# A conditioned EMA block and a top-k FFN on one core: where the scores are made, warm-up matmuls, and a new order of steps

## The reference, cut to what matters

```python
ctx    = ema(x, tau_ctx)                                  # scan over the 32 tokens
wg     = sigmoid([x, ctx] @ Wg.T + bg);  gated = x * wg
mod    = 0.5 + sigmoid(gelu(x @ Wn1.T + bn1) @ Wn2.T + bn2)   # 128 modes
temporal = sum_d softmax(blend)[d] * ema(gated * mod[d], tau[d])
gate   = sigmoid(temporal @ Wtemp.T + btemp)
y      = layernorm((gelu(x @ Wsoma.T + bsoma) * gate) @ Wout.T) * gamma + beta
scores = y @ w_router
top 16 of the 32 tokens of each sequence:
    out[token] = y[token] + sigmoid(score) * (gelu(y[token] @ W1 + b1) @ W2 + b2)
result = x + out
```

## Time and profile before

| | |
|---|---|
| median of three runs | 192.11 us (189.43, 192.11, 192.43) |
| the profiled execution | 189.27 us, its span 187.5 us |
| mean granted clock of TensorE | 0.991 of full speed |
| TensorE matmuls busy | 172.6 us, 92% |
| VectorE / GpSimd / ScalarE busy | 143.6 / 134.8 / 96.5 us |

### The profile page before, as it was taken

How to read it: one execution, slowest core, us unless ns; L and a number is a source line. 1 busy time by engine, 2 the same in 40 slices (tenths; PEclk the granted TensorE clock), 3 DMA queues, 4 the chain that set the end, 5 groups by cost and what they waited for, 6 DMA issues and landing times.

```text
span 187.5 us, 3480 instructions
## 1 busy us (share of the span) xinstructions
PE 172.6 (92%) x1154; PEld 130.4 (70%) x1154; DVE 143.6 (77%) x223; ACT 96.5 (51%) x177; POOL 134.8 (72%) x158
## 2 busy tenths in 40 slices
PE   5798999999999999999999999999999983994991
PEld 4485445877669588695769687688689943983881
DVE  1628897769997988859787887798789749858822
ACT  3548697264680141772505454578487465157030
POOL 7838000788897999979686988999797599529800
PEclk9999999999999999999999999999999997899999
DMA  5687000000000000000000000000002000303032
GB/s 128 167 209 201 0 3 0 0 2 5 0 0 0 3 0 3 0 0 0 3 2 0 0 3 2 0 0 3 2 0 59 0 2 0 112 3 112 0 112 59
DMA packets 12785, 5.62 MB, mean 30 GB/s; under 512 B 2880, under 2 KB 12640, under 8 KB 12768
## 3 DMA queue, kind: packets, MB, share of 16 engines
q1 hardware_dynamic: 11904, 5.20, 10.3%
q10 hardware_dynamic: 864, 0.20, 0.5%
HBM read 3.30 MB, written 2.10 MB: 29 GB/s over the span
## 4 chain that ended last, share of the span: by engine, by line
PE 76%; DVE 11%; issue 3%; POOL 3%; ACT 2%; DMA 2%; ACTq 0%; DVEq 0%; POOLq 0%
PE ring L1042 27%; PE ring L1109 6%; PE ring L1015 5%; PE ring L1026 4%; PE ring L999 4%; PE ring L978 4%; PE ring L1000 4%; PE ring L1049 4%; DVE small L842 3%; PE ring L1057 3%; DVE spread L846 3%; PE ring L1006 2%; PE ring L1032 2%; PE ring L992 2%; PE ring L966 2%
## 5 line engine op out<-in xcount | busy, mean ns | idle before, releaser
L468 POOL TENSOR_TENSOR ctx_acc<-ctx_acc,prod 128x256 f32<-128x256 f32 (+17 forms) x75 | 81.0, 1095 | 30.9 <-DVE prod L817 26.8
L817 DVE TENSOR_TENSOR prod<-ring,gm 128x256 f32<-128x256 f32 (+17 forms) x75 | 41.3, 577 | 8.9 <-PE ring L1042 7.4
L1042 PE MATMUL ring<-mod_hi,decayed_lo 128*128 128x512 f32 (+15 forms) x104 | 35.0, 374 | 0.0
L1042 PE MATMUL ring<-mod_lo,decayed_hi 128*128 128x512 f32 (+15 forms) x104 | 30.1, 326 | 0.0
L1042 PE MATMUL ring<-mod_hi,decayed_hi 128*128 128x512 f32 (+15 forms) x104 | 30.0, 327 | 0.0
L1042 PEld LDWEIGHTS ring<-mod_hi,decayed_lo 128*128 128x128 f32 x104 | 18.4, 189 | 7.6 <-issue 6.3
L1042 PEld LDWEIGHTS ring<-mod_lo,decayed_hi 128*128 128x128 f32 x104 | 19.2, 189 | 2.0 <-issue 1.2
L1042 PEld LDWEIGHTS ring<-mod_hi,decayed_hi 128*128 128x128 f32 x104 | 19.2, 189 | 0.9
L804 DVE TENSOR_TENSOR state<-ring,blend_w 128x1024 f32<-128x1024 f32 x16 | 18.8, 1219 | 1.1 <-PE ring L1015 0.9
L1109 PE MATMUL ring<-w_sb,gm 128*128 128x128 f32 x128 | 15.8, 282 | 0.1
L1109 PEld LDWEIGHTS ring<-w_sb,gm 128*128 128x128 f32 x128 | 15.4, 199 | 0.3 <-issue 0.3
(11 more groups left out here) (168 smaller groups left out, 358.9 us busy)
## 6 DMA issues: line engine op xcount, KB each, us to landing
x_nat<-in_x_dram SPq DMA_DIRECT2D x3, 512.0 KB, 4.2
out_dram<-x_nat SPq DMA_DIRECT2D x3, 512.0 KB, 3.2
x_nat<-in_x_dram SPq DMA_DIRECT2D x2, 256.0 KB, 4.7
w_sb<-in_L_ffn_W_dram SPq DMA_DIRECT2D x2, 256.0 KB, 5.3
out_dram<-x_nat SPq DMA_DIRECT2D x2, 256.0 KB, 3.2
down<-in_cond_dram SPq DMA_DIRECT2D x2, 64.0 KB, 2.7
prod<-in_L_cond_Wg_dram ACTq DMA_DIRECT2D x1, 128.0 KB, 2.8
prod<-in_L_cond_Wsoma_dram ACTq DMA_DIRECT2D x1, 64.0 KB, 2.9
```

Source lines behind the costliest of these rows:

```text
L468: nc.gpsimd.tensor_tensor(dst, dst, packed(prod[:, n % NP, 0:width(r)], r, k), ALU.add).then_inc(acc_done, 1)
L817: nc.vector.tensor_tensor(dst, packed(slot(step), r, k), lagged(gated(r), r, k), ALU.mult).then_inc(read(step), 1)
L1042: last = nc.tensor.matmul(to[:, c], w[:, k, :], src[:, c], start=(i == 0), stop=(i == len(parts) - 1))
```

## The change

1. Scores: `var` on GpSimd no longer adds 1e-5 in an instruction of its own; `squares` has a 129th column that holds 1e-5, and the sum takes it in. GpSimd makes the score product right after the power. `score` on VectorE copies the product into PSUM and makes `spread` from there; `pick_w` likewise reads its sigmoid from a copy in PSUM. The step `score` now takes the bank, and `bc` uses the same one; the equality test overwrites the spread scores there, after the greater-than test instead of before it. The bank comes free after `pick_w` instead of after `pick`.
2. `normed` on ScalarE waits for the power, scales `o_sb` first and does the tanh last.
3. Warm-up matmuls: 5 before the steps, 1 after `turn_b`, 4 after `turn_a`.
4. The four DMAs of `bn1` are issued ahead of `bias_in` and of x of round 1. The biases are halved in step `soft`.
5. A new `ORDER`.

```diff
-WARM = 3
+WARM = (5, 1, 4)
 ORDER = """
+decay:0 powers:0 xt:0 turn_b:0 turn_a:0 h1:0 context:0 mod:0 soft:0 turn_c:0 xt:1 wg:0 xt:2 decays:0
+context:1 xt:3 context:2 split:0 h1:1 wg:1 gated:0 rw:0 context:3 turn_f:0 gated:1 table:0.0 table:0.1
...
+unit:4.2 unit:4.6 up:1.0 state:4.0 plus_beta:1 gate:3 up:1.1 score:2 normed:2 residual:1 soma_gate:3
+unit:4.4 turn_pick:1 bc:2 tie:2 pick:2 down:1 out:3.0 stats:3.0 gather:2 out:3.1 stats:3.1 var:3 unit:4.8
+unit:4.15 carry:4.0 up:2.0 back:4.0 up:2.1 sum:4 score:3 normed:3 bc:3 scatter:1 turn_pick:2 tie:3
+plus_beta:2 pick:3 gate:4 soma_gate:4 down:2 gather:3 residual:2 out:4.0 stats:4.0 scatter:2 var:4
+plus_beta:3 up:3.0 score:4 up:3.1 residual:3 normed:4 bc:4 turn_pick:3 plus_beta:4 tie:4 pick:4 down:3
+gather:4 scatter:3 up:4.0 up:4.1 turn_pick:4 down:4 residual:4 scatter:4
...
+        def scores(r, i):
+            return slot(("score", r, 0))[:, NT * T + i * NT:][:, 0:tiles(r)]
...
+            for g in range(BT):
+                sp.dma_start(bn1[g * HN:(g + 1) * HN, :], col(b_n1)).then_inc(bn1_in, 16)
             sp.dma_start(bias_in[:, 0:1], col(b_g)).then_inc(bias_inn, 16)
             sp.dma_start(bias_in[:, 1:2], col(b_n2)).then_inc(bias_inn, 16)
             sp.dma_start(tiles_of(x_nat, 1), tiles_of(x_dram, 1)).then_inc(x_in[1], 16)
-            for g in range(BT):
-                sp.dma_start(bn1[g * HN:(g + 1) * HN, :], col(b_n1)).then_inc(bn1_in, 16)
...
                 elif kind == "var":
-                    nc.gpsimd.tensor_scalar(small[..4..], small[..5..], 1e-5, None, ALU.add)
-                    nc.gpsimd.tensor_tensor(small[..7..], small[..4..], minus_half[..], ALU.pow)
+                    nc.gpsimd.tensor_tensor(small[..7..], small[..5..], minus_half[..], ALU.pow)
+                    pool.wait_ge(rstd_done, r + 1)
+                    for h in range(QUADS[r]):
+                        pool.wait_ge(read(("out", r, h)), reads_after(("out", r, h)))
+                    nc.gpsimd.tensor_tensor(small[..6..], o_sb[:, r % 2, 0:tiles(r), E], small[..7..], ALU.mult)
...
                 elif kind == "score":
-                    dve.wait_ge(rstd_done, r + 1)
-                    nc.vector.tensor_tensor(s[6], o_sb[:, r % 2, 0:tiles(r), E], s[7], ALU.mult)
+                    for former in FORMER[step]:
+                        dve.wait_ge(read(former), reads_after(former))
                     dve.wait_ge(score_done, r + 1)
+                    nc.vector.tensor_copy(scores(r, 0), small[:, r % 2, 6, 0:tiles(r)])
                     nc.vector.tensor_tensor(spread[:, 0:tiles(r), :], eye_t[..],
-                                            s[6][:, :, None].to_broadcast([P, tiles(r), T]), ALU.mult)
+                                            scores(r, 0)[:, :, None].to_broadcast([P, tiles(r), T]), ALU.mult)
...
                 elif kind == "pick":
+                    nc.vector.tensor_copy(scores(r, 1), small[:, r % 2, 9, 0:n])
                     nc.vector.scalar_tensor_tensor(out=pick_w[:, 0:n, :],
-                        in0=small[:, r % 2, 9, 0:n][..], scalar=1.0,
+                        in0=scores(r, 1)[:, :, None].to_broadcast([P, n, SEL]), scalar=1.0,
                         in1=pick[:, 0:n, 0:SEL], op0=ALU.add, op1=ALU.mult)
...
+                if kind in ("turn_b", "turn_a"):
+                    warm_up(WARM[1 if kind == "turn_b" else 2])
```

More of the change, by code:

```diff
@@ L59 @@
 ORDER = """
[L60 to L79, removed]
@@ L80 @@
-soma_gate:4 normed:3 turn_pick:2 plus_beta:2 pick:3 down:2 plus_beta:3 residual:2 out:4.0 gather:3 stats:4.0
-var:4 scatter:2 turn_pick:3 up:3.0 up:3.1 score:4 bc:4 normed:4 tie:4 pick:4 down:3 plus_beta:4 residual:3
-gather:4 scatter:3 up:4.0 residual:4 up:4.1 turn_pick:4 down:4 scatter:4
+decay:0 powers:0 xt:0 turn_b:0 turn_a:0 h1:0 context:0 mod:0 soft:0 turn_c:0 xt:1 wg:0 xt:2 decays:0
+context:1 xt:3 context:2 split:0 h1:1 wg:1 gated:0 rw:0 context:3 turn_f:0 gated:1 table:0.0 table:0.1
+table:0.2 wg:2 low:0 gated:2 table:0.3 mod:1 split:1 low:1 wg:3 gated:3 early:0 unit:0.0 h1:2 unit:0.8 h1:3
@@ new lines @@
+turn_d:0 unit:0.12 unit:0.1 unit:0.7 nat:0.0 unit:0.14 unit:1.0 unit:1.13 early:1 unit:1.14 unit:1.6 ffn_w:0
+unit:0.13 mod:2 turn_e:0 unit:1.7 plus_beta:0 unit:0.5 unit:1.15 nat:1.0 unit:0.4 state:0.0 unit:0.2 soma:0
+unit:1.1 unit:0.6 unit:0.10 state:1.0 soma:1 unit:0.9 carry:0.0 unit:0.11 unit:1.8 unit:0.15 unit:0.3
+split:2 low:2 back:0.0 sum:0 mod:3 nat:1.1 unit:1.2 unit:2.0 unit:2.13 unit:1.11 state:1.1 unit:2.9 gate:0
+soma_gate:0 unit:2.1 unit:1.5 unit:1.3 early:2 nat:2.1 out:0.0 unit:2.2 xt:4 context:4 unit:1.10 carry:1.1
@@ new lines @@
+state:2.1 unit:1.9 carry:1.0 unit:2.8 back:1.1 unit:1.12 nat:2.0 h1:4 stats:0.0 unit:2.11 early:3 unit:1.4
+state:2.0 split:3 low:3 carry:2.1 back:1.0 soma:2 unit:2.7 nat:3.0 unit:2.12 unit:3.0 unit:2.14 unit:3.5
+nat:3.1 unit:2.6 unit:3.15 sum:1 unit:3.1 state:3.1 unit:2.3 carry:2.0 unit:3.8 unit:2.4 var:0 state:3.0
+gate:1 back:2.1 carry:3.1 soma_gate:1 unit:2.15 unit:2.5 back:2.0 unit:2.10 unit:3.10 mod:4 split:4 wg:4
+low:4 score:0 out:1.0 gated:4 unit:3.13 unit:4.0 unit:4.10 unit:4.5 sum:2 stats:1.0 bc:0 back:3.1 normed:0
@@ new lines @@
+unit:3.2 tie:0 out:1.1 stats:1.1 var:1 unit:4.7 pick:0 unit:3.14 unit:3.9 gate:2 soma_gate:2 carry:3.0
+gather:0 unit:3.7 unit:3.4 residual:0 unit:4.13 up:0.0 up:0.1 back:3.0 turn_pick:0 score:1 down:0 bc:1 tie:1
+normed:1 unit:3.11 unit:3.3 soma:3 unit:4.12 pick:1 out:2.0 unit:4.1 unit:4.14 early:4 stats:2.0 unit:4.9
+unit:3.12 soma:4 unit:4.11 out:2.1 unit:3.6 nat:4.0 sum:3 unit:4.3 gather:1 scatter:0 stats:2.1 var:2
+unit:4.2 unit:4.6 up:1.0 state:4.0 plus_beta:1 gate:3 up:1.1 score:2 normed:2 residual:1 soma_gate:3
@@ L632, in _ @@
                 elif kind == "normed":
[L633 to L637, removed]
+                    act.wait_ge(rstd_done, r + 1)
+                    for h in range(QUADS[r]):
+                        act.wait_ge(read(("out", r, h)), reads_after(("out", r, h)))
                     for n in range(tiles(r)):
@@ L870, in _ @@
                     n = tiles(r)
-                    made = ("bc", r, 0)
                     if r:
@@ L926, in _ @@
                 kind, r, k = step
-                if step not in FIRST:
+                if kind == "bc":
+                    pe.wait_ge(spread_done, r + 1)
+                    nc.tensor.matmul(slot(("score", r, 0))[:, 0:tiles(r) * T],
+                                     same_b[:, :, :].rearrange("p b t -> p (b t)"),
+                                     spread[:, 0:tiles(r), :].rearrange("p n u -> p (n u)"),
+                                     start=True, stop=True).then_inc(full(("score", r, 0)), 1)
+                if step not in FIRST or kind == "score":
                     continue
```

75 lines of the change are left out of this document (38 added, 37 removed).

## The result

The changed kernel took 182.19 us in the median of four runs (180.9 to 183.08), the kernel before 191.91: ratio 0.953, 95% interval 0.9415 to 0.9645. The profiled execution took 182.02 us with a span of 180.2, where the kernel before had 189.27 and 187.5: 7.3 us less. The forecast was 183.3 us.

The account below looks back on a forecast made before the run. TensorE's own work bounds the kernel, leaving 14.9 idle us, mostly at the ends. Gains of 6.0 + 1.5 + 1.3 = 8.8 us take the median from 192.11 to 183.3 us (profiled execution 180.5); range 180.0 to 189.5.

Parts of the forecast that it names:

- What bounds: Whole kernel: TensorE busy 172.6 of 187.5 us, full from 30.60 to 150; the change can act only at both ends.
- Part 1: Score chain at the end, rounds 3 and 4: shorter chain closes TensorE's gaps and the slow stretch, 7.5 us gained.
- both gaps: TensorE's idle time ahead of `bc:3` (3.72 us) and `bc:4` (2.75 us), together 6.47; both could close, 6.0 us booked.
- the slow stretch behind `bc:3`: From `bc` to the end of `down`, 6.14 us against 4.65 in round 2; without the gap, 1.5 us more gained.
- The 0.5 us kept for what might stay: Idle time allowed to remain ahead of `bc:3` and `bc:4` together, taken off 6.47 us to give 6.0.
- Rival A: Score chain: the small PSUM copy or the mask product still waits for GpSimd, 4 us lost, 187.3 us; chance 0.14.
- Part 2: Head: ten warm-up matmuls bring TensorE's faster pace forward, and bn1 loads earlier; 1.3 us gained.
- The delay that I put at 1.2 us: Head: net delay from the added warm-up matmuls, set against 2.5 us won by the faster pace.
- what is late next: x of round 1: Head: this load lands at 9 to 12 us, wanted at about 11 by `xt:1`; could take the head's whole gain back.
- Part 3: Order in the middle: same TensorE steps, so 0 gained, with 0 to 3 us of possible loss.
- Rival B: Head gains nothing or loses 1 us, middle loses 2 to products waiting for GpSimd; 187.6 us, chance 0.18.
- rival C: Rounds 1 to 3: `score` waits for GpSimd's queued product, no banks come free, TensorE stops; 199 us, chance 0.06.

Follow-up runs that it names:

- experiment 4: Changed kernel with both score products back on VectorE from SBUF, the 1e-5 add still gone: 187.31 us, ratio 0.9862 to the kernel before.
- experiment 5: Changed kernel with the mask product reading the scores from SBUF instead of the PSUM copy, the copy staying: 183.44 us, ratio 0.9566 to the kernel before.
- experiment 2: Kernel before with the new order alone, old score steps, warm-up and DMAs: 194.2 us, ratio 1.014.
- experiment 1: Kernel before with the new score code (later tanh and bias halving included), three score steps moved later in the old order: 191.38 us, ratio 1.0.
- experiment 3: As experiment 1, but with four of the five score steps moved so that banks are given out late enough: 185.27 us, ratio 0.9753 to the kernel before.
- experiment 6: Changed kernel with the old warm-up, three matmuls instead of ten: 181.12 us, ratio 0.953 to the kernel before.
- experiment 7: Changed kernel with the load of x of round 3 issued right behind x of round 2: 178.0 us, ratio 0.9306 to the kernel before.
- experiment 8: Kernel of experiment 7 with three warm-up matmuls instead of ten: 181.02 us, ratio 0.9519 to the kernel before.
- experiment 9: Kernel before with ten warm-up matmuls and bn1's DMAs ahead of the biases, old order and scores: 190.73 us, ratio 0.985.

## Why the prediction was right, point by point

**What bounds.** The view that the ends and not the middle hold the time was right for the result: the middle is full in both kernels, and on the chain that ended last it is 156.9 us from the first unit to the end of the span before and 148.8 after, 8.1 less:

```profile
30.60 2.00 PE ring L1042 x12
...
31.43 0.69 PE ring L1063 x3
```

The first line is from the kernel before, the second from the changed one.

**Part 1, the score chain.** Forecast 7.5 us. The terms held one by one: product on GpSimd 0.20 (I took 0.23), copy 0.17 (0.16), mask product 0.42 and 0.29 as taken, both gaps closed, the slow stretch behind `bc:3` gone (`down:2` 3.73 us). The 0.5 us kept for what might stay was not needed. Experiments 4 and 5 show the mechanism, with the waits put back in round 4. Rival A falls: each of the ten copies into PSUM took 0.15 to 0.17 us.

**What part 1 left out.** It booked the gap ahead of `bc:3`, 3.72 us and the 1.5 of the slow stretch behind it, to the scores alone. By experiments 2 and 4 the new order closes this gap too, with the products still on VectorE. The change does both, so the sum came out, but 5.2 of the 7.5 us can't be given to one of the two.

I wrote that the held bank harms nothing since its next users stand a `down` later. For the new list that is true. But I set the order down as a part worth nothing, and it is what lets part 1 pay: experiments 1 and 2 show that the new scores in nearly the old list give 1.0 and the new list with the old scores 1.014, and only placed banks (experiment 3) free the gain. With that kernel against experiment 6, same warm-up and same chip, the rest of the order, with bn1's DMAs moved, is worth 4.2 us by the medians (185.27 and 181.12). In the profiled executions, where that of experiment 3 was its slowest, TensorE is busy for 173.3 us instead of 170.3, in part since it was slowed once behind a gap, and idle for 11.7 instead of 8.6. The terms don't add up; they depend on each other.

**Part 2, the head.** The failing term: forecast a gain of 1.3 us, measured 0.8 lost at the first unit (31.43 instead of 30.60), and 1.3 with the steps that moved across it counted (`h1:2`, 0.57, and `turn_d`, 0.12, went behind; `turn_f`, 0.22, came ahead). The warm-up did what was said of it, in the changed kernel's timeline:

```profile
7.95 0.42 PE L1006 MATMUL ring<-x_t,turned_w 128*32 128x128 f32 x8
...
10.15 1.09 PE L987 MATMUL ring<-ident,x_nat 128*128 128x128 f32 x8
```

The transposes of `xt:1` took 1.09 us instead of 1.91, and did not wait for x of round 1. The delay that I put at 1.2 us was 0.2 (`h1:0` at 7.95 instead of 7.73), so up to there the warm-up won more than forecast. The step that failed is "what is late next: x of round 1". It was x of round 3, which the old list hid behind a slow TensorE and `h1:1`; the new list puts `xt:3` first. I had not asked where `xt:3`, too, would stand once TensorE was 2 us early, nor that the wait would give the pace back: 2.82 us idle, then 4.1 us at 0.58. Experiments 7 and 8 show both.

**Part 3.** 0 forecast, 0 found in the full stretch. Rival B had the size of the head right (nothing, or 1 us lost), though not which load it was, and the middle wrong; rival C didn't occur in the changed kernel, though experiment 1 is a cousin of it, a bank held by the score chain that stops TensorE for 4 us in a step that has nothing to do with it.

**The size.** 8.8 us forecast, 7.3 in the profiled executions (8.1 from the first unit on, less 0.8 in the head), 9.0 by the ratio, 9.7 between the medians. The profiled execution of before, 189.27, lies at the fast edge of its runs, and the changed kernel's runs spread less; so the trace explains 7.3 us, and the rest is the spread of before, whose cause I did not look for. That the median came within 1.1 us of 183.3 is partly luck. I had added to the forecast for the profiled execution the 2.84 us by which the median of before lies above its own; the changed kernel's lies 0.17 above. The forecast for the profiled execution, 180.5, was 1.5 us too low, and the head's loss instead of a gain, 2.1 us, is more than all of it.

## What to carry to other kernels

Where steps share a ring of banks, an order, the moment at which a step takes its bank and the moment at which it lets go are one thing: measure them together, and look in the trace for a matmul that waits for an engine whose result it never reads. A small product on VectorE that lies on the path should have one of its two inputs in PSUM while GpSimd is at work; a copy of four or eight values into PSUM buys that for 0.17 us. Before you book a gap to one edit, ask whether another edit of the same change closes it too: here the new order did. When an engine gets faster at the start, list every load by the time at which it will now be wanted, not only the next one: here one load, moved by four places in the queue, was worth some 4 us beside ten warm-up matmuls and nothing beside three, and the further matmuls were worth nothing without it.

## What the runs showed of the hardware

- Up to 13 us the profile gives a granted clock of 1.00 throughout, while the eight transposes of `xt:1` took 1.91 us with three warm-up matmuls (before, experiments 6 and 8) and 1.04 to 1.09 with ten. For the start, the durations say what the clock row does not. In the changed kernel the pace changed within the warm-up:

```profile
1.59 2.50 PE L936 MATMUL ring<-ident 128*128 128x128 f32 x10 [1.59 <-POOL ident L400]
...
6.87 1.11 PE L936 MATMUL ring<-ident 128*128 128x128 f32 x8
```

That is 0.25 us for each instruction and then 0.14.

- Short waits brought the clock down in some places and not in others. It was 0.58 for 4.1 us behind 2.82 us of idle time (the changed kernel) and 0.72 for 6 us around 1.44 us of it (experiment 3), but 1.00 behind 2.75 us (before, 172.69 to 178), behind 1.76 us (experiment 9), and in the same 6 us around the same wait of 1.44 us in experiment 1. How long the wait is does not decide it alone.
